# Sorted rows in two halves, the last eight units' first halves scattered ahead, and two expert stages interleaved at their joint

## What is computed

```python
x = x + attn(layernorm(x));  x = x + xattn(layernorm(x), ctx, ctx)
h = layernorm(x)
swiglu(h, w1, w2, w3) = silu(h @ w1.T) * (h @ w3.T) @ w2.T      # 128 -> 352 -> 128
p, e = top1(sigmoid(clip(h @ router_w.T + bias, -50, 50)))       # one of 7 experts
tw   = clip(0.5 + p + 1e-8, 0.5, 2.0)
out  = x + 0.5 / tw * swiglu(h, shared) + p / tw * swiglu(h, expert[e])
```

## Time and profile before

| | us |
|---|---|
| median of 3 runs | 498.48 |
| lowest, highest | 492.63, 499.39 |
| the profiled execution | 490.89 |
| its span, first to last instruction | 489.0 |

### The profile page before, as it was taken

One profiled execution on the slowest core, in us unless ns is written; L12 is line 12 of the kernel. 1 busy time (PEld: TensorE's weight loads), 2 busy tenths in 40 slices (PEclk: granted clock), 3 DMA queues, 4 the chain that ended last, 5 costly groups with the idle time before them and its releaser, 6 DMA issues. The chain is left out here.

```text
span 489.0 us, 16657 instructions
## 1 busy us (share of the span) xinstructions
PE 428.8 (88%) x5528; PEld 320.9 (66%) x5529; DVE 321.0 (66%) x959; ACT 292.4 (60%) x695; POOL 281.7 (58%) x461
## 2 busy tenths in 40 slices
PE   1786989998998999999999987689999589999990
PEld 0344556665564665666666654579999479999990
DVE  5346878987786988888989875276555324455441
ACT  2335868886785787878787874312222236666660
POOL 5965657686585686868686844214544404444442
PEclk9998999999898999999999998599999969999997
DMA  5265434464453555443433332001111244540000
GB/s 98 44 123 97 85 50 68 74 119 73 65 104 59 92 103 96 69 77 37 77 37 35 69 32 74 2 8 68 65 65 65 78 108 132 139 115 23 30 32 6
DMA packets 173598, 34.11 MB, mean 70 GB/s; under 512 B 146387, under 2 KB 170966, under 8 KB 173536
## 3 DMA queue, kind: packets, MB, share of 16 engines
q1 hardware_dynamic: 160480, 19.50, 26.3%
q10 hardware_dynamic: 10304, 7.47, 5.3%
q0 software_dynamic: 2752, 6.33, 3.7%
HBM read 19.83 MB, written 15.41 MB: 72 GB/s over the span
## 5 line engine op out<-in xcount | busy, mean ns | idle before, releaser
L877 DVE TENSOR_TENSOR gT<-gT,bank 128x384 f32<-128x384 f32 x70 | 38.7, 554 | 68.2 <-PE bank L562 56.6
L424 POOL DMA_INDIRECT out<-yrow,token x38 | 37.3, 983 | 55.0 <-DVE yrow L991 43.2
L724 ACT ACTIVATE gT<-bank 128x384 f32<-128x384 f32 x70 | 34.1, 487 | 53.0 <-PE bank L562 51.4
L792 DVE TENSOR_REDUCE mx_x<-bank 128x8 f32<-128x512 f32 x64 | 43.9, 686 | 29.0 <-PE bank L444 29.0
L389 POOL TENSOR_TENSOR k_s<-pT,hmask_sb 128x1024 f32<-128x1024 f32 x32 | 60.9, 1903 | 3.3 <-ACT pT L695 3.3
L571 PE MATMUL bank<-wdn_sb,gT 128*128 (+1 forms) x420 | 58.8, 276 | 2.9 <-DVE rowb L887 2.3
L562 PE MATMUL bank<-fhT,wtile 128*128 128x128 f32 x456 | 59.8, 283 | 0.0
L415 POOL DMA_INDIRECT sorted_rows<-rowb,place x32 | 31.0, 968 | 44.8 <-DVE rowb L887 32.4
L562 PEld LDWEIGHTS bank<-fhT,wtile 128*128 128x128 f32 x456 | 56.4, 199 | 0.2 <-issue 0.2
L571 PEld LDWEIGHTS bank<-wdn_sb,gT 128*128 128x128 f32 x420 | 52.8, 193 | 3.8 <-DVE gT L877 2.7
L355 POOL TENSOR_SCALAR xn_s<-x_all,mv 128x128 f32<-128x128 f32 x32 | 19.4, 607 | 62.1 <-DVE mv L784 61.0
(11 more groups left out here) (135 smaller groups left out, 894.5 us busy)
## 6 DMA issues: line engine op xcount, KB each, us to landing
ring<-sorted_rows SPq DMA_DIRECT2D x38, 129.0 KB
sorted_rows<-nowhere_row SPq DMA_DIRECT2D x9, 516.0 KB, 4.2
wup_sb<-in_wup ACTq DMA_DIRECT2D x8, 352.0 KB, 3.5
ring<-in_ctxv SPq DMA_DIRECT2D x64, 32.0 KB, 3.3
attention_out<-on_s SPq DMA_DIRECT2D x64, 32.0 KB, 3.5
orow<-attention_out SPq DMA_DIRECT2D x32, 64.0 KB, 1.8
x_all<-in_x ACTq DMA_DIRECT2D x3, 512.0 KB, 4.3
cross_keys<-in_ctxk ACTq DMA_DIRECT2D x6, 256.0 KB, 4.6
```

The costliest lines, as they stand in the source:

```text
L424: pool.indirect_dma_start(out=out, out_offset=bass.IndirectOffsetOnAxis(ap=token[p][:, 0:1], axis=0), in_=yrow[p][:, :], in_offset=None, b ...
L724: nc.scalar.activation(gT[p][:].rearrange("p c q -> p (c q)"), ps_gate[p][:, 0:CH * P], ACT.Silu).then_inc(sem("f_act"), 1)
L792: nc.vector.tensor_reduce(mx[k][:, g, :], scores_of(k, g), AX.X, ALU.max).then_inc(sem(f"{k}_mx"), 1)
L877: nc.vector.tensor_tensor(g, g, ps_up[p][:, 0:CH * P], ALU.mult).then_inc(sem("f_g"), 1)
```

## The change

The row of a token becomes two halves of 130 floats: first h, the routed weight and the token number, then x plus the shared part and two unused floats. The token's row is assembled in place: `x_all`, `h_all` and the two numbers become slices of one array `rows_all`, DVE's result goes straight into it, and the three copies, the four `rowb` buffers and the wait for a free one go away. Places are cast to integers once for all units, with separate tables for the scatters of halves.

Units 24 to 31 are scattered as halves. Their first halves, which exist since phase A, go out from POOL between the whole rows of units 0 to 21, one every third unit; their second halves go out when the shared result is there. SP loads the first halves of slots 0 to 7 once units 0 to 23 and the eight first halves have landed, their second halves once the second halves of the last units have landed, and whole rows from slot 8 on. For slots 0 to 3, DVE writes the weighted routed result alone and POOL adds the second half before the output scatter.

On PE, ACT and DVE the last two shared units are interleaved with the first routed slots. The queues there, in rows that name line, operation and operands (`bank6`/`bank7` are the outputs of `down`, `bank4`/`bank5` of the transposes, `bank0` to `bank3` of `up`; `fx` and `fhT` the slot's h and its transpose).

The diff, cut to what bears on these stages:

```diff
-ROW = 2 * D + 2
-WT, TOK = 2 * D, 2 * D + 1
+HALF = D + 2
+ROW = 2 * HALF
+WT, TOK = D, D + 1
+LATE = 24
+SPLIT = 8
+PATCHED = 4
...
-            load(sp, hs_all[:, 0, :], hs_tiles[:, 0, :], "c_row0")
-            load(sp, hs_all[:, 1, :], hs_tiles[:, 1, :], "c_row1")
...
+            sp.wait_ge(sem("b_sent"), 16 * LATE)
+            sp.wait_ge(sem("h_sent"), 16 * (U - LATE))
+            for s in range(SPLIT):
+                if s >= 2:
+                    sp.wait_ge(sem(f"c_row{s % 2}"), 16 * (s // 2))
+                load(sp, hs_all[:, s, 0:HALF], hs_tiles[:, s, 0:HALF], f"c_row{s % 2}")
+            sp.wait_ge(sem("x_sent"), 16 * (U - LATE))
+            for s in range(SPLIT):
+                load(sp, hs_all[:, s, HALF:ROW], hs_tiles[:, s, HALF:ROW], f"c_x{s}")
...
+            for n in range(U):
+                if n < LATE and n % 3 == 0:
+                    scatter(hs_halves, place_h, n // 3, rows_all[:, LATE + n // 3, 0:HALF], "h_sent")
+                pool.wait_ge(sem("f_y"), at(n))
+                if n < LATE:
+                    scatter(hs_dram, place, n, rows_all[:, n, :], "b_sent")
+                else:
+                    scatter(hs_halves, place_x, n - LATE, rows_all[:, n, HALF:ROW], "x_sent")
...
+            for s in range(PATCHED):
+                pool.wait_ge(sem("f_y"), at(s + U))
+                pool.wait_ge(sem(f"c_x{s}"), 16)
+                nc.gpsimd.tensor_tensor(yrow[s][:], yrow[s][:], hs_all[:, s, HALF:HALF + D], ALU.add).then_inc(sem("patched"), 1)
+                pool.wait_ge(sem("patched"), s + 1)
+                put_rows(s)
...
             to_hT(0, 0)
+            down(U - 2, 0, E)
             to_hT(1, 1)
             routed_up(0, 0)
+            down(U - 1, 1, E)
             to_hT(2, 0)
             routed_up(1, 1)
...
             tile_weights(0, 0)
+            silu(U - 2, 0)
+            routed_hT(0, 0)
             tile_weights(1, 1)
-            routed_hT(0, 0)
+            silu(U - 1, 1)
             routed_hT(1, 1)
             silu(U, 0)
...
-                nc.vector.tensor_copy(rowb[q][:, 0:D], h_all[:, n, :])
-                nc.vector.tensor_copy(rowb[q][:, WT:ROW], meta[:, n, :])
...
                 nc.vector.scalar_tensor_tensor(
-                    rowb[q][:, D:2 * D], ps_y[p], r1["c1"][:, n:n + 1] if isinstance(n, int) else r1["c1"][:, bass.ds(n, 1)],
+                    x_all[:, n, :], ps_y[p], r1["c1"][:, n:n + 1] if isinstance(n, int) else r1["c1"][:, bass.ds(n, 1)],
                     x_all[:, n, :], ALU.mult, ALU.add).then_inc(sem("f_y"), 1)
...
-            for s in range(3):
-                routed_in(s, s % 2, 16 * (s // 2 + 1))
+            routed_in(0, 0, 16)
+            b_step(U - 2, U - 2)
+            routed_in(1, 1, 16)
+            routed_in(2, 0, 32)
+            shared_row(U - 2, 0)
+            shared_row(U - 1, 1)
             gated(U, 0)
             routed_in(3, 1, 32)
```

More of the change, by code:

```diff
@@ L136, in build @@
         ps_r = bank[6][:, 512 - U * E:].rearrange("p (u e) -> p u e", e=E)
-        rowb = [sb(f"rowb{i}", [P, ROW]) for i in range(NROW)]
-        place = [sb(f"place{i}", [P, 1], I32) for i in range(NROW)]
+        place = sb("place", [P, U], I32)
+        place_h = sb("place_h", [P, U - LATE], I32)
+        place_x = sb("place_x", [P, U - LATE], I32)
         token = [sb(f"token{i}", [P, 1], I32) for i in range(NROW)]
@@ L411, in _, with scatter, put_rows @@
             pool.wait_ge(sem("prefilled"), 16 * ((SLOTS + CHUNK - 1) // CHUNK))
[L413 to L414 removed]
+            pool.wait_ge(sem("x_xn"), U)
+            pool.wait_ge(sem("weight_steps"), N_WEIGHT)
+            pool.wait_ge(sem("placed"), 3)
+            def scatter(table, where, n, rows, name):
                 pool.indirect_dma_start(
[L416 to L423 removed]
+                    out=table, out_offset=bass.IndirectOffsetOnAxis(ap=where[:, n:n + 1], axis=0),
+                    in_=rows, in_offset=None).then_inc(sem(name), 16)
+            for n in range(U):
[6 more added lines that the diff above has]
+                    scatter(hs_halves, place_x, n - LATE, rows_all[:, n, HALF:ROW], "x_sent")
+            def put_rows(p):
                 pool.indirect_dma_start(
@@ L427, in put @@
                     bounds_check=NTOK - 1, oob_is_err=False).then_inc(sem(f"c_put{p}"), 16)
-            steps(pool, put, SLOTS, 0, SLOTS % NROW, turn=NROW)
+            def put(s, p):
+                wait_apart(pool, ("f_y", at(s + U)))
+                put_rows(p)
+            for s in range(PATCHED):
[4 more added lines that the diff above has]
+                put_rows(s)
+            with pool.Fori(0, (SLOTS - PATCHED) // NROW) as i:
+                for k in range(NROW):
+                    put(i * NROW + (PATCHED + k), (PATCHED + k) % NROW)
+            for s in range(SLOTS - (SLOTS - PATCHED) % NROW, SLOTS):
+                put(s, s % NROW)
             for q in range(NROW):
@@ L579, in shared @@
                 down(n, p, E)
-                if not (isinstance(n, int) and n + 2 >= U):
-                    shared_up(n + 2, p)
+                shared_up(n + 2, p)
             shared_up(0, 0)
@@ L919, in _ @@
             gated(0, 0)
-            b_step(0, 0, None)
+            b_step(0, 0)
             weights = [
```

94 lines of the change are left out of this document (48 added, 46 removed).

## The result

Twenty runs of each kernel: the changed one has a median of **499.07 us** (495.27 to 504.32), the kernel before 495.78 (491.30 to 499.61), ratio **1.0083 [1.0051, 1.0114]**. The median of before is 2.7 us under the three runs that I had; the forecast saving of 7.6 would have made 488.2 of it, so the miss is 10.9 us.

The account below looks back on a forecast made before the run. PE was taken to bound both stages, with a 7.34 us hole at the joint. Saving 9.3 us there less 1.7 for low clock, all else 0, gave 498.5 - 7.6 = 490.9 us, range 483 to 496.

Parts of the forecast that it names:

- The joint: Between shared and routed stage: the 7.34 us PE hole shrinks, 9.3 us saved at full clock, 7.6 with the clock's fall.
- the wait: At the joint, PE waits a new 2.6 us, from 384.42 to 387.0, ahead of transpose 1.
- The clock: At the joint's 2.6 us gap the clock falls, leaving 7.6 us saved; rival that it holds, 9.3 saved, chance 0.33.
- The price: Behind the joint's gap, some 3.4 us of low clock costs PE 1.7 us, bounds 0 to 3.4.
- the shared stage at 0: Shared stage: only PE's queue counts, extra POOL scatters leave no backlog and cost nothing; no change in its length.
- both periods: Shared unit and routed slot keep their times on PE, 2.01 and 2.12 us.
- The rival for "slower": Shared stage: half-row scatters make POOL the bound above 2.2 us each, slower in all from 3.8 us each; chance 0.04.
- The routed stage: Behind the joint: POOL's adds take 1.8 us per slot, under the 2.12 period, no backlog; cost 0, bound 0.2.
- The halves' loads: First halves are loaded with 5 us to spare and second halves in time; late chances 0.05 and 0.08.

Follow-up runs that it names:

- halves_ahead: Changed kernel with all eight first-half scatters sent ahead of unit 0's: 487.5 us, 0.9825 of the kernel before (chip 3).
- spaced: Changed kernel with a small POOL memset and a wait behind each scatter up to unit 23: 487.5 us on chip 3, 497.1 on chip 6.
- narrow_halves: Changed kernel with first halves scattered as 16 floats per row to their own array, inputs of units 24 to 31 left out: 488.8 us, 0.9873 (chip 3).
- narrow_again: Same kernel as narrow_halves, run on chip 10: 499.8 us, 0.9924 of the kernel before.
- four_late: best with four units in halves instead of six, first halves ahead of units 2, 8, 14 and 20: 492.2 us, 0.9839 of the kernel before (chip 0).
- best: six_late plus turned ACT and DVE orders at the joint and no POOL adds: 488.8 us, 0.9867 (chip 10); 492.1 us, 0.9980 (chip 0).
- six_late: Changed kernel with six units in halves instead of eight, first halves four units apart: 494.7 us, 0.9967 of the kernel before (chip 10).
- before_extra: Kernel before with eight extra 128x128 scatters to an unread array: 495.8 us, 1.0008 on chip 3; 509.8 us, 1.0265 on chip 6.

## Why the prediction was wrong

**The joint: right.** The steps, their order and the size held: 8.0 us saved with the clock's fall (forecast 7.6), and 9.66 without it (forecast 9.3) in `halves_ahead`, `spaced` and others at 8.67. Only the wait was 0.6 shorter. That the measured 8.0 lies so near 7.6 is in part luck: it needed the clock to fall in the execution that was profiled.

**The clock: a coin, and forecast as one.** Among the thirteen profiles with the changed order at the joint and this gap of 2.0 us, it fell in six (joint 10.3) and stayed in seven (8.7). One kernel did both: `narrow_halves` fell, and as `narrow_again`, on another chip, it stayed. `four_late`, with a gap of 2.00 behind other work, stayed. The windows of `halves_ahead`, empty stretch and what came behind, beside those of after above:

```profile
393.00:395.00 2.00, 0.07 (x1) 0.00 (x0) 0.95 (x4) 1.01 (x2) 0.00 (x0) 1.00 0.10 33
396.00:399.00 3.00, 3.00 (x29) 3.00 (x28) 0.95 (x3) 1.82 (x4) 2.00 (x3) 1.00 0.13 44
```

The price, 10.3 - 8.7 = 1.6, is the forecast 1.7. Removing the gap (`best`) is worth both: it does not throw the coin. The prediction sorted its rows by the length of the gap, and the trace of before has rows that break that order: the clock stayed at 1.00 behind 3.26 us without PE work (from 9.58) and behind 1.84 (from 60.93, which it read as near 1.6), and fell to 0.50 behind 1.34 (from 120.67). The length of the gap alone does not decide.

**The failed step: the shared stage at 0.** The prediction said that in this stage "only the PE queue counts", that "PE does not wait for POOL in the shared stage, so only the joint moves", and took both periods as unchanged; it asked of the eight extra scatters only what POOL pays for them, with 2.2 us each as the point where POOL becomes the bound. POOL pays 0.96 and never bounded anything. But scatters close behind one another hold the next start on ACT and DVE, and that holds PE: +9.3 us where 0 stood, with nothing in my bounds for it. The rival for "slower" had the right place and the wrong mechanism: it went through POOL's time and the joint, not through other engines. The rest of the change did cost 0 in this stage: with the same rows, tables and place conversions `halves_ahead` took 67.32 on chip 3.

Could the profile have told? The trace of before has scatters 2.01 us apart there, a few near 1.5 at the start, and one run, the last three (385.78, 387.05, 388.31), in the hole, where nobody was waiting. So no row showed the price of a run, and I had priced the extra scatters by the engine that issues them alone.

**The routed stage: +2.0 instead of 0.** From `up` of slot 2 to the last `up` it takes 74.06 us before and 75.38 after, 1.3 more. That is the POOL adds together with the same effect: on chip 10 this stretch takes 75.33 with them (`six_late`) and 74.24 without (`best`), and on chip 3, with them, 74.06 (`spaced`). In after, one patched slot takes POOL 2.2 us, not 1.8, since 0.79 lies between add and scatter where I had 0.1; it falls behind, and the next two scatters run together:

```profile
415.48 0.43 POOL L464 TENSOR_TENSOR yrow<-yrow,ring 128x128 f32<-128x128 f32 x1
...
416.70 0.99 POOL L452 DMA_INDIRECT out<-yrow,token  x1 [0.79 <-POOL yrow L464]
...
418.13 0.97 POOL L452 DMA_INDIRECT out<-yrow,token  x1 [0.44 <-issue]
...
418.91 0.56 DVE L921 TENSOR_TENSOR gT<-gT,bank 128x384 f32<-128x384 f32 x1 [1.63 <-PE bank L604]
```

`gated` is due at 418.37 here and starts at 418.91. The other 0.7 lies behind the end of the last output scatter: from there to the span's end it is 7.36 us before and 8.07 after. `before_extra` has 8.07 too, so it comes with the extra scatters and not with the layout; `best` with six has 7.88, `four_late` with four 7.69, but `six_late` 8.30. What stands there is open. The halves' loads were in time, as forecast.

**What is not settled.** That runs of scatters hold ACT and DVE on chips 0, 6, 8 and 10 and not on chip 3 is shown, in one session on each. No kernel went back to chip 3, so whether it is the chip or something that each session sets up anew stays untested. How the scatters hold the others is not shown. The starts in question fit a picture in which each scatter leaves some 1.48 us of work behind, one after the other, and a signal to ACT or DVE waits for it: the run of four from 343.75 ends at 343.75 + 4 x 1.48 = 349.67, where Silu starts at 349.62; the run of three from 360.31 ends at 364.75, `gated` at 364.68; the run from 331.18, six, at 340.06, Silu at 340.00. That is an arithmetic fit, and no row shows the work itself. Nor can I say what differs in chip 3. The Trainium skill, on its page SBUF — State Buffer, section "SBUF: two separate sides", lets only VectorE and GpSimd contend for a shared port pair, with ScalarE waiting for nobody; Silu on ACT is the first to be late at 349.62, so that rule does not explain this delay. Its page Perfetto Trace Analysis, section "DMA Instruction — SWDGE (GPSIMD)", has the recorded time of such an issue end when the descriptors are made, not when the data has moved; this case agrees as far as it can, with 0.96 us for 64 bytes a row as for 1 KB.

## What to carry to other kernels

Price an added operation by everyone who is near it, not only by the engine that issues it: a duration in its row says what it costs there and nothing about whom it holds. If the trace shows an operation only spaced out, treat a run of it as an operation without a row, and give it a bound on the slow side. When several different cures all work, suspect what they share, here the chip or its session, and repeat the sick case beside them before believing any.

## What the runs showed of the hardware

- Indirect scatters of 128 rows, issued 1.26 us apart in runs of three or more, make Silu on ACT or `gated` on DVE start late, by up to 1.45 us behind three (`four_late`), 2.4 behind four and 3.2 behind six (the changed kernel), on four chips of five that were tried with them (0, 6, 8, 10; one session each), and on the fifth (3) not at all, with 23 in a row. Spaced 2.01 us, as behind the last extra scatter, they cost nothing on any; spaced 1.46 they still cost 8 us of this stage on chip 6.
- The bytes of the extra scatters do not matter: with rows of 64 bytes and of 520 bytes the stage took the same (76.29 and 76.46 on chip 10).
- Behind a gap of 2.0 us in PE's work the granted clock fell to its lower level (0.53 over 401 to 404) in six profiles and stayed at 1.00 in seven with the same gap. In the kernel before it stayed behind 1.84 and 3.26 us and fell behind 1.34.
